# Folding mirrored image rows and filter taps behind the row transform of a convolution by 2-D Fourier transforms

## The reference, cut to what matters

```python
def _L0_conv_ref(x, ...):                    # x is the group-normalised input, (8, 56, 56, 256)
    xn = simple_rms(x)
    u = silu(xn @ W_u.T + b_u)               # 512 wide
    v = silu(xn @ W_v.T + b_v)               # 512 wide, 8 heads of 64
    g = rpe_coeffs(...)                      # a small MLP over the 111 x 111 offsets, 512 wide
    a = zeros((8, 112, 112, 64)); a[offsets modulo 112] = g
    vf = rfft2(v, s=(112, 112)); af = rfft2(a)
    y = irfft2(vf * af, s=(112, 112))[..., :56, :56, :]
    return (u * y) @ W_o.T + b_o + x
x = x + _L0_conv_ref(_gn(x), ...)
```

## Time and profile before

| | |
|---|---|
| median of 3 runs | 5410.76 us (5406.27 to 5413.85) |
| profiled execution, first to last instruction | 5398.1 us |
| PE busy | 5214.1 us (97%) |
| PEld busy | 3662.3 us (68%) |
| DVE busy | 3997.7 us (74%) |
| ACT busy | 2512.3 us (47%) |
| POOL busy | 2489.9 us (46%) |
| moved by DMA | 782.62 MB, mean 145 GB/s |

### The profile page before, as it was taken

The page is one execution under the profiler, slowest core; times in us unless marked ns, Lnnn a source line. Parts: engine busy times, 40 slices in busy tenths (PEclk is TensorE's granted clock), DMA queues, the critical chain, the costliest instruction groups (busy, mean ns, idle before and its releaser), DMA issues. The chain is left out here.

```text
span 5398.1 us, 89326 instructions
## 1 busy us (share of the span) xinstructions
PE 5214.1 (97%) x27048; PEld 3662.3 (68%) x27048; DVE 3997.7 (74%) x6176; ACT 2512.3 (47%) x4791; POOL 2489.9 (46%) x1381
## 2 busy tenths in 40 slices
PE   8999899997999999999998999999989999987999
PEld 6777655554555555555556777777767777765999
DVE  6777666666999999999996676766635666665887
ACT  5555577774434334343434555555532222211555
POOL 0000054443999999999995555555301111111332
PEclk9999999998999999999999999999999999998999
DMA  3222167775444444444446666666533333433443
GB/s 109 89 89 72 53 197 219 217 217 170 149 150 150 149 152 148 152 148 150 151 136 182 195 203 200 191 200 202 163 113 97 104 113 107 118 89 97 123 122 113
DMA packets 349121, 782.62 MB, mean 145 GB/s; under 512 B 43433, under 2 KB 147845, under 8 KB 339460
## 3 DMA queue, kind: packets, MB, share of 16 engines
q1 hardware_dynamic: 326596, 703.91, 44.2%
q10 hardware_dynamic: 22400, 77.08, 4.0%
HBM read 420.49 MB, written 360.38 MB: 145 GB/s over the span
## 5 line engine op out<-in xcount | busy, mean ns | idle before, releaser
L928 POOL TENSOR_TENSOR co_prod<-co_cross 111x512 f32<-111x512 f32 x448 | 848.8, 1895 | 0.0
L862 ACT ACTIVATE co_y_out<-co_y_ps 112x512 f32<-112x512 f32 x448 | 267.9, 598 | 928.2 <-PE co_y_ps L808 923.1
L925 POOL TENSOR_TENSOR co_prod<-co_direct 111x512 f32<-111x512 f32 x448 | 576.3, 1286 | 203.8 <-PE co_y_ps L808 116.0
L902 DVE TENSOR_TENSOR co_direct<-co_v_ps,co_spec 111x1024 f32<-111x1024 f32 x448 | 543.5, 1213 | 92.0 <-PE co_v_ps L135 87.9
L2012 POOL TENSOR_TENSOR at_t<-at_t,at_p_bias 112x1024 f32<-112x1024 f32 x56 | 137.7, 2470 | 889.3 <-DMA at_t<-t_tiles 889.3
L904 DVE TENSOR_TENSOR co_cross<-co_v_ps,co_spec 111x1024 f32<-111x1024 f32 x448 | 541.5, 1209 | 0.0
L135 PE MATMUL co_v_ps<-co_v_high,co_col_fwd_high 112*111 112x512 f32 x896 | 506.1, 565 | 1.4 <-DVE co_cross L904 1.4
L806 PE MATMUL co_y_ps<-co_prod,co_col_inv 111*112 111x512 f32 x896 | 458.2, 592 | 0.0
L808 PE MATMUL co_y_ps<-co_prod,co_col_inv 111*112 111x512 f32 x896 | 457.5, 592 | 0.1
L882 DVE TENSOR_TENSOR co_v_low<-co_v_in,co_v_high 112x1024 fp32r<-112x1024 f32 x224 | 372.3, 1662 | 0.0
L135 PE MATMUL co_v_ps<-co_v_low,co_col_fwd_high 112*111 112x512 f32 x896 | 354.3, 395 | 0.0
(11 more groups left out here) (277 smaller groups left out, 14268.5 us busy)
## 6 DMA issues: line engine op xcount, KB each, us to landing
v_rows<-pr_rows_out SPq DMA_DIRECT2D x56, 1792.0 KB, 8.2
co_v_in<-v_rows SPq DMA_DIRECT2D x448, 224.0 KB
y_rows<-co_y_out SPq DMA_DIRECT2D x448, 224.0 KB
mx_y_in<-y_rows SPq DMA_DIRECT2D x224, 448.0 KB, 5.5
kr_x_in<-x SPq DMA_DIRECT2D x56, 448.0 KB, 3.9
kern_rows<-kr_rows_out SPq DMA_DIRECT2D x28, 896.0 KB, 4.7
pr_x_in<-x SPq DMA_DIRECT2D x112, 224.0 KB
mx_x_in<-x SPq DMA_DIRECT2D x56, 448.0 KB, 5.3
```

What stands on the lines that cost most here:

```text
L862: nc.scalar.activation(y_out[:, b, :], y_ps[b % 2][:2 * SIDE, :], ACT.Copy).then_inc(y_ready, 1)
L902: nc.vector.tensor_tensor(direct[b % 2][:], v_ps[b % 2][:POINTS, :], spec[i][:, :2 * WIDE], ALU.mult).then_inc(real_terms, 1)
L925: nc.gpsimd.tensor_tensor(prod[b % 2][:, :WIDE], direct[b % 2][:, :WIDE], direct[b % 2][:, WIDE:], ALU.subtract).then_inc(real_ready, 1)
L928: nc.gpsimd.tensor_tensor(prod[b % 2][:, WIDE:], cross[b % 2][:, :WIDE], cross[b % 2][:, WIDE:], ALU.add).then_inc(combined, 1)
```

## The change

The 56 image rows are taken in mirrored order: the host hands x over with its rows permuted so that a chunk of 8 rows holds rows and their mirror images, in turns of two rows and the two that mirror them, and permutes the result back. A transform over positions that are mirrored about the middle needs only the sum of a pair for its cosines and the difference for its sines. So the sums and differences ("folds") are taken once, behind the row transform, and the column transform works on 56 real numbers per part where the old one needed the complex matrix of 112 by 112. The filter taps are folded in the same way, tap p with tap -p.

- Kernel rows: GpSimd folds each set of four rows by an add and a subtract of 1024 elements each, after casting the next points; the store becomes three DMAs, since real and imaginary parts of the differences change places.
- Project: ScalarE copies the first tile of a pair out of PSUM, two banks at once; VectorE adds and subtracts the second tile, 1024 elements each; three DMAs store the rows. The normalised x is stored to HBM by two DMAs a chunk, and GpSimd waits for that store before it overwrites the buffer.
- Columns: no splits. The forward transform is two fp32 matmuls in the two halves of the array's rows, the inverse two fp32 matmuls in the two halves of its columns, the spectrum two fp32 matmuls. VectorE multiplies once with 2048 elements (v is read twice by a broadcast), GpSimd adds once with 1024. The inverse lies three images behind; terms and products have four buffers each.
- Mix: the normalised x is loaded instead of computed. The two tiles of a pair out of the inverse row transform are unfolded: ScalarE copies the second tile, VectorE adds and subtracts, GpSimd multiplies with the gate (four ops of 512). PE's list is rearranged.

The diff, cut to its core:

```diff
-                        sp.wait_ge(row_out, s * TAIL + RPE_ROWS * (u + 1))
-                        at = (s * 2 + u) * RPE_ROWS
-                        sp.dma_start(d["kern_rows"][:, at:at + RPE_ROWS, :], rows_out[u][:]).then_inc(stored[u], 16)
+                        sp.wait_ge(folded, 2 * (s * 2 + u + 1))
+                        at = (s * 2 + u) * MIRRORS
+                        sums, diffs = slice(at, at + MIRRORS), slice(FREQ + at, FREQ + at + MIRRORS)
+                        real, imag = slice(0, FREQ), slice(FREQ, ROWS)
+                        sp.dma_start(d["kern_rows"][:, sums, :], taps_out[u][:, :MIRRORS, :]).then_inc(stored[u], 16)
+                        sp.dma_start(d["kern_rows"][real, diffs, :], taps_out[u][imag, MIRRORS:, :]).then_inc(stored[u], 16)
+                        sp.dma_start(d["kern_rows"][imag, diffs, :], taps_out[u][real, MIRRORS:, :]).then_inc(stored[u], 16)
...
+                def fold_rows(s, u):
+                    n = s * 2 + u
+                    pool.wait_ge(row_out, RPE_ROWS * (n + 1))
+                    pool.wait_ge(stored[u], 16 * PIECES * s)
+                    pair = rows_out[u][:].rearrange("p (m r) n -> p m r n", r=2)
+                    for parity, op in enumerate((ALU.add, ALU.subtract)):
+                        nc.gpsimd.tensor_tensor(taps_out[u][:, parity * MIRRORS:(parity + 1) * MIRRORS, :], pair[:, :, 0, :],
+                                                pair[:, :, 1, :], op).then_inc(folded, 1)
+
                 for s in range(STEPS):
                     for u in range(2):
                         take_points(s, u)
+                        if s:
+                            fold_rows(s - 1, u)
...
-        LAG = 2
+        LAG = 3
...
+                def spectrum(k, part):
+                    if part == 0:
+                        pe.wait_ge(taps_loaded, k * 32 + 32)
+                        pe.wait_ge(spec_ready, k)
+                    last = nc.tensor.matmul(taps_ps[:POINTS, bass.ts(part, WIDE)], col_taps[:, part, :], taps_in[:, part, :],
+                                            start=True, stop=True)
+                    if part == 1:
+                        last.then_inc(taps_mm, 1)
 
                 def forward(k, b):
                     n = k * BATCH + b
-                    pe.wait_ge(low_v, k * PAIRS + b // 2 + 1)
-                    buffer_free(pe, multiplied, n)
-                    for out in range(2):
-                        last = product(nc, v_ps[b % 2][:POINTS, bass.ts(out, WIDE)], [w[:, out, :] for w in col_fwd],
-                                       [x[:, b, :] for x in v], start=True, stop=True)
+                    pe.wait_ge(v_loaded[b // 2], k * 32 + 32)
+                    wait_slot(pe, multiplied, n)
+                    for part in range(2):
+                        side = slice(part * GAP, part * GAP + SIDE)
+                        last = nc.tensor.matmul(v_ps[b % 2][:POINTS, bass.ts(part, WIDE)], col_fwd[side, :], v_in[side, b, :],
+                                                start=True, stop=True)
                     last.then_inc(fwd_mm, 1)
...
+                        for part in range(2):
+                            last = nc.tensor.matmul(y_ps[b % 2][part * GAP:part * GAP + SIDE, :],
+                                                    col_inv[:, part * SIDE:(part + 1) * SIDE],
+                                                    prod[b % RING][:, bass.ts(part, WIDE)], start=True, stop=True)
+                    last.then_inc(inv_mm, 1)
...
-                        if b == BATCH // 2 + 1 and more:
-                            spectrum(k + 1)
+                        if more and b <= LAG + 1:
+                            spectrum(k + 1, b - LAG)
                         forward(k, b)
                         inverse(k, b - LAG)
...
-                def split_v(k, pair):
-                    act.wait_ge(v_loaded[pair], k * 32 + 32)
-                    images = slice(2 * pair, 2 * pair + 2)
-                    nc.scalar.activation(v[0][:, images, :], v_in[:, images, :], ACT.Copy).then_inc(high_v, 1)
...
-                        nc.vector.tensor_tensor(direct[b % 2][:], v_ps[b % 2][:POINTS, :], spec[i][:, :2 * WIDE],
-                                                ALU.mult).then_inc(real_terms, 1)
-                        nc.vector.tensor_tensor(cross[b % 2][:], v_ps[b % 2][:POINTS, :], spec[i][:, WIDE:],
-                                                ALU.mult).then_inc(multiplied, 1)
...
+                        twice = [POINTS, 2, 2 * WIDE]
+                        nc.vector.tensor_tensor(terms[b % RING][:].rearrange("p (t n) -> p t n", t=2),
+                                                v_ps[b % 2][:POINTS, :].unsqueeze(1).to_broadcast(twice),
+                                                spec[i][:].rearrange("p (t n) -> p t n", t=2), ALU.mult).then_inc(multiplied, 1)
...
+                    for b in POOLED:
+                        pool.wait_ge(multiplied, SLOTS + k * BATCH + b + 1)
+                        wait_inverse(pool, k, b - RING)
+                        pair = terms[b % RING][:].rearrange("p (t s n) -> p t s n", t=2, s=2)
+                        nc.gpsimd.tensor_tensor(prod[b % RING][:].rearrange("p (t n) -> p t n", t=2), pair[:, :, 0, :], pair[:, :, 1, :],
                                                 ALU.add).then_inc(combined, 1)
...
+                    sp.wait_ge(folded, 1 + (GROUP * s + j + 1) * PAIRS)
+                    rows, out, stored = rows_of_chunk(d["v_rows"], GROUP * s + j), rows_out[j % 2], rows_stored[j % 2]
+                    real, imag, sums, diffs = slice(0, FREQ), slice(FREQ, ROWS), slots(0, 0, HALF_ROWS), slots(1, 0, HALF_ROWS)
+                    sp.dma_start(rows[:, sums, :], out[:, sums, :]).then_inc(stored, 16)
+                    sp.dma_start(rows[real, diffs, :], out[imag, diffs, :]).then_inc(stored, 16)
+                    sp.dma_start(rows[imag, diffs, :], out[real, diffs, :]).then_inc(stored, 16)
+
+                def store_gx(s, j):
+                    rows = d["gx_rows"][GROUP * s + j]
+                    for r in range(2):
+                        sp.dma_start(rows[r], gx[j][r * GAP:r * GAP + SIDE, :, :]).then_inc(gx_stored[j], 16)
...
+                    sp.wait_ge(gx_ready, s * GROUP + j + 1)
                     if left >= GROUP:
-                        sp.wait_ge(gx_ready, s * GROUP + j + 1)
                         load(s + 1, j)
+                    store_gx(s, j)
                     if j % 2 == 0:
                         store_inv(s, j // 2)
                     store_rows(s, j)
...
+                        pool.wait_ge(gx_stored[j], s * 32)
...
+                def take_first(s, j, pair):
+                    n = (s * GROUP + j) * PAIRS + pair
+                    act.wait_ge(row_mm, 2 * n + 1)
+                    act.wait_ge(folded, n)
+                    nc.scalar.activation(first[pair][:], row_ps[0][:ROWS, :], ACT.Copy).then_inc(first_out, 1)
...
+                    dve.wait_ge(first_out, 1 + n + 1)
+                    dve.wait_ge(row_mm, 2 * n + 2)
...
+                    nc.vector.tensor_tensor(out[:, slots(0, pair), :].rearrange("p r n -> p (r n)"), first[pair][:],
+                                            row_ps[1][:ROWS, :], ALU.add)
+                    nc.vector.tensor_tensor(out[:, slots(1, pair), :].rearrange("p r n -> p (r n)"), first[pair][:],
+                                            row_ps[1][:ROWS, :], ALU.subtract).then_inc(folded, 1)
...
+                def mix(g, t):
+                    n = g * TILES + t
+                    pool.wait_ge(unfolded, n + 1)
+                    pool.wait_ge(gate_ready, n + 1)
+                    nc.gpsimd.tensor_tensor(gated[t][:], gated[t][:], gate[t][:], ALU.mult).then_inc(gated_ready, 1)
...
                 def step(before3, before2, before, now, after, later):
                     if now:
+                        inverse_rows(*now, 0)
+                        inverse_rows(*now, 1)
                         gate_mm(*now, 2)
                     if before:
+                        turn_gated(*before, 3)
                         output_mm(*before, 2)
-                        turn_gated(*before, 3)
                     if after:
                         pe.wait_ge(low_x, number(after) * HALVES + 1)
                         turn_x(*after, 1)
                     if now:
-                        inverse_rows(*now, 0)
-                        inverse_rows(*now, 1)
                         gate_mm(*now, 3)
+                        turn_gated(*now, 0)
+                        inverse_rows(*now, 2)
+                        inverse_rows(*now, 3)
                     if before:
                         output_mm(*before, 3)
-                    if now:
-                        turn_gated(*now, 0)
...
+                def take_odd(s, u, pair):
+                    n = (s * 2 + u) * (TILES // 2) + pair
+                    act.wait_ge(y_mm, 2 * n + 2)
```

(10 more changed lines are left out.)

450 lines of the change are left out of this document (208 added, 242 removed).

## The result

The changed kernel takes 5426.3 us (median of 20 runs, 5401.42 to 5442.87), the kernel before, on the same chips, 5407.15 us: a ratio of 1.0034, 95% interval 1.0025 to 1.0043. It is slower by a third of a per cent, where 6.5% faster was forecast. The profiled execution has a span of 5415.7 us, against 5398.1 us before.

The account below looks back on a forecast made before the run. PE was taken as the bound, in columns with VectorE close behind. Columns -463, project +62, kernel rows +50 sum to -351 on 5398.1 us: 5047, plus 12.7 for launch and end, 5060 us; range 4940 to 5200.

Parts of the forecast that it names:

- Columns, the gain: Columns stage: pace falls from 3.434 to 2.40 us an image, GpSimd slowest at 2.38, loads staying ahead; -463 us.
- The first rival: Columns: PE paces, each change between array halves costing 0.33 us, 2.70 us an image; 135 us more, 5195; chance 0.20.
- Project, a cost: Project stage: storing the normalised x lengthens a circle of waits, 11.65 us a chunk against 10.51; +62 us.
- The circle: Project: waits through SP, DMA, GpSimd and ScalarE, 0.66 us to spare before; forecast 23.2 us per two chunks.
- The third rival: Project: transfers fill the stage, 1 KB pieces perhaps at half rate; 13.0 us a chunk, +134 us, 5130; chance 0.10.
- Kernel rows, a cost: Kernel rows: GpSimd's folds delay VectorE's low halves, PE 3.2 us late in each of 14 steps; +50 us.
- Mix, nothing: Mix stage: engines have room and PE's other work hides the new copy, sum and product chain; no change, bounds -5 and +56.
- The slower one: Fourth rival, columns: alternating matmul pairs do not share the array, PE needs 3.74 us an image; 5660 us; chance 0.04.

Follow-up runs that it names:

- all mends: Changed kernel plus earlier taps load, reordered ScalarE lists in project and mix, SP's list turned in project, casts before four-piece folds: 4961.39 us, ratio 0.9175.

## Why the prediction was wrong, step by step

**Columns, the gain.** The pace itself was right: 2.40 us forecast, 2.33 measured once the taps are in time, with PE, VectorE and GpSimd full together (1034, 991 and 1038 of 1040 us), and a gain of 1558.9 - 1066.9 = 492 us where 463 was forecast. The step that failed is the sentence "Loads stay ahead: this stage moves 148 GB/s now and would need 148 x 3.434/2.40 = 212". It asked whether the bytes get through, and they do (219 GB/s); it did not ask when SP issues them. In SP's list the taps load moves from the second pair of a row (`pair == 1`) to the last (`pair + 1 == PAIRS`), behind a store that waits, while the spectrum that reads the taps moves forward, from image 5 of the row to images 3 and 4. The prediction counted loads and did not place them. This cost 223 us, almost half the gain. Its two signs of being wrong, a pace above 2.7 us (2.83) and gaps on PE in mix, both came.

One reading of the kernel before is off without consequence: two inverse transforms with a spectrum between them start 5.89 us apart (2005.49 and 2011.38), so the spectrum adds 2.80 us and not 3.17. That is why the 3.49 us of PE work an image lies above the 3.434 measured.

The first rival, changes between halves of the array, is answered by the timeline of the changed kernel: a forward and an inverse with a change behind each take 2.05 us (2000.09 to 2002.14), of which 1.72 are the forecast's two times 0.86. By this estimate a change costs 0.16 to 0.17 us, under the 0.19 that the forecast allowed for each pair and half of the rival's 0.33. The Trainium skill (TensorEngine Tiling (Array Packing), Key Properties) says that changing the tiling mode drains the TensorE; the trace agrees that there is a cost and shows it to be small here.

**Project, a cost.** The mechanism was the wrong one, though the signs that it named (GpSimd waiting for DMA, ScalarE for GpSimd) were there. The failed step is "PE does not mind: VectorE has 368 of 560 us busy and gains about 2 us per 10.5". A share of 0.66 that becomes 0.85 leaves no room for 1.8 us of waiting twice a chunk, and where the copy stands in ScalarE's list was not followed. The circle that was followed instead is there (GpSimd's wait of 8.09 us), but it binds only once the chain is gone, and then by 10 us. The third rival's premise, that pieces of 1 KB may go at half the rate, is shown by no run: the same stores are among the transfers that reach 249 GB/s.

**Kernel rows, a cost.** Right in kind: GpSimd's folds hold up VectorE's low halves. The size was off because of "the other fold falls among the layers, where I leave the VectorE chain its slack": there, two operations stand still too (2.18 and 2.29 us against 0.25 and 0.22), PE waits 14.7 us for the statistics behind them, and the step is 5.5 us longer (77/14), not 3.2. A part is the clock, which the forecast left out: PE's busy time per record is 0.143 us (606.97/4246) against 0.139 before (592.04/4259), by estimate 19 of the 77 us. The Trainium skill (SBUF — State Buffer, Who interferes with whom) says that a VectorE instruction with two SBUF inputs contends with a GpSimd instruction that reads SBUF, that a copy or cast in a two-port mode can contend with GpSimd too, and that whichever starts first keeps the shared ports for its whole length while the other is fully blocked. The trace agrees in this: those that stand still read SBUF alone, the cast of 112 elements included, and the coefficient at 370.94, which reads PSUM, takes its usual 0.74 us within the fold. Which mode the cast ran in, no run shows.

**Mix, nothing.** The failed step is "between the inverse rows and the first turn PE now has two gate passes [...] which hide it". That cover was counted against 2.6 us of copy, sum and product. It did not count what stands ahead of the copy in ScalarE's list (2.8 us for a bias and a table load), nor that the products hold up VectorE's shift. Measured +107 us; two moves in one list give back 82. Of the last 25 us the cause stays open. With all mends PE is busy for 871 of 880 us of the stage, which leaves some 11 us of idleness over its whole length; the rest lies in PE's busy time per record, 0.157 us (871.21/5564) against 0.154 before (900/5827). The rearranged order of PE's list was not tried by itself.

**The rivals.** None of them came. The slower one had the right sign by a mechanism that is refuted: a pair of transforms takes 2.05 us, not 3.44. The time came from waits in all four stages. Those of columns, project and mix are a matter of order in a list; that of kernel rows is VectorE held up beside GpSimd's folds.

## What to carry to other kernels

When work is taken off the engine that sets the pace, every list of the others is to be read again from its waits: a load, copy or cast that was early enough behind something else may now be the last to come. An edit's cost is not only the duration of its instructions but also the place where they stand: here, moving a handful of loads, copies and casts ahead of things that they do not need, and cutting the folds in pieces, turned 1.0034 into 0.9175. When one wait is removed and the time does not move, look for the wait that it had covered before giving up the cause, as with the folds in pieces.

## What the runs showed of the hardware

After a wait of 3.43 us PE's next two groups ran near the lower clock level (1.97 and 1.90 us for what takes 1.11). Not every wait had this behind it: after those of 2.44 and 2.49 us ahead of 2014.04 and 2035.27 the next two groups took 1.11. In the stage 146 us of waits cost 223. GpSimd's operations in pieces let VectorE in between: its longest blocked low half went from 2706 to 1219 ns, at 0.74 us a piece and 6.5 us for eight against 5.2 for two. Pairs of fp32 matmuls that alternate between row halves and column halves of the array cost 0.16 to 0.17 us a change, by the estimate above.
